# Placeholder rows written in bulk, rank products in another PSUM bank, a second buffer for turned tokens

## The chip, the cores and the metric

One core of a Trainium2 chip runs the whole program as one launch. The metric is device time in microseconds (us), the median of the runs of the kernel. The core has five engines: TensorE (PE in the profile), VectorE (DVE), ScalarE (ACT), GpSimd (POOL) and SyncE (SP). SP and POOL issue the DMAs, and these run on the core's 16 DMA engines.

## What is computed

The input is 8 images of 16 x 16 tokens with 192 channels, all in float32. Four blocks follow each other, each with a layer norm before it and a residual after it:

```
x = x + window_attention(ln(x))            # 14 x 14 windows, 12 heads, relative positions
t = t + gelu(ln(t) @ W_in + b) @ W_out      # dense feed-forward, 192 -> 768 -> 192
x = x + afno(ln(x))                         # rfft2, two block-diagonal complex layers, irfft2, plus a bias layer
t = t + moe(ln(t))                          # top 2 of 8 experts by softmax of gate logits
# moe: token -> its two experts' gelu(x @ w1[e] + b1[e]) @ w2[e] + b2[e], weighted by the two shares
```

## The kernel before, in words

The 2048 tokens are 16 tiles of 128 rows, in 4 groups of 4 tiles (GROUPS = 4; a group is two images). Every engine has its own instruction stream, written out by hand, and the streams meet only in semaphores. The order of the work is thus the order of the lines of each engine.

**Stages.** Attention comes first. The dense feed-forward stage is the loop with `hidden_layer` and `output_layer`. The AFNO stage is `forward`, `first_layer`, `second_layer`, `inverse` on PE, one pass for each group. The mixture-of-experts stage (MoE) overlaps it: while PE does group `it` of the AFNO stage, in `mixing(it)`, the gate of group `it - 1` is worked out. `turn_rows` and `gates` give the logits, DVE picks two experts for each token in `chosen` (a chain of small instructions in which each waits for the one before), `ranks` multiplies the 0/1 choice matrix by a triangular matrix and by ones to count tokens, and `slots` on DVE turns counts into slot numbers.

**The store of expert rows.** `xs_d` lies in HBM. It has a region of CAP = 2176 rows for each of the NE = 8 experts, and 128 more rows at FREE. A row has DX = 196 floats (784 B): 192 values of the token, its place and its shares. POOL's `scatter` (L596) writes every token's row to the slots of its two experts by indirect DMA, 8 DMAs for each group. Then each tile of 128 slots is an expert tile: SP loads it (`load_rows`, L475), PE turns it (`turn_x`, L1762), ACT copies the turned tile from PSUM bank 0 to `xst` (`turned`, L638), PE makes the first layer (`first`, L1793 and L1798), ACT the gelu (L801), PE the second layer (`second`, L1807), DVE bias and weight (`result`, L1257 to L1268), and POOL adds the 128 rows to the output in HBM by an indirect accumulating DMA (L623). There are NTILE = 39 such tiles. EARLY = 9 of them are started from the tokens of the first two groups, before the later groups have slots.

**Placeholder rows.** An expert's last tile is not full. Its rest must hold rows whose place points to a dump row of the output. Before the change, SP writes 128 placeholder rows behind the last taken slot of each expert, in `free_rows` (L477 to L480): it reads the slot from `next_i`, which DVE writes after the last group's slots (L1321), and copies 128 x 196 floats from the input `free_rows` to `xs_d`. These are 8 DMAs from HBM to HBM, four after the load of tile 6 and four after the load of tile 7. SP waits for them (`free_in`) ahead of the load of tile EARLY.

**Banks.** For groups 0 to 2 the gate's PSUM bank is 0 and the rank products lie in bank 1; for the last group they are banks 6 and 7. `turn_blocks` (L1592) writes banks 0 and 1, so PE waits for DVE's `slots` (g_slot) ahead of it in passes 1 and 2. `forward` writes banks 2 to 5.

**SP's order** around the change: small tables, then w1e and w2e of the eight experts (16 DMAs of some 577 KB, L457 and L458), b2e (L459), the dump rows of the output (L460), `store_residual(0)` and `(1)` (L465), a wait for the scatters of groups 0 and 1 (sc0), loads of tiles 0 to 3, `store_residual(2)` and `(3)`, loads of tiles 4 and on. **POOL's order**: scatter of groups 0, 1, 2, then the 39 additions, with the scatter of group 3 put between additions 2 and 4.

Of the kernel before, what the change touches and what calls it, by code (L numbers as in the profile page):

```python
# [13 lines left out]
I32 = mybir.dt.int32  # L14
ALU = mybir.AluOpType
# [32 lines left out]
NE = 8  # L48
# [24 lines left out]
def metaformer(nc, a, out):  # L73
    with ExitStack() as ctx:
# [140 lines left out]
        v8 = {n: down("e_" + n, [P, NE]) for n in ("next", "cnt", "full", "padded", "end", "begin", "taken", "start", "hop")}  # L215
        next_i = down("next_i", [P, NE], I32)
        above = down("above", [P, NE, 16])
# [12 lines left out]
        xtm = down("xtm", [C, 2, 512])  # L230
        xst = down("xst", [P, 2, P])

# [63 lines left out]
        def gate_bank(group):  # L296

            return 6 if group == GROUPS - 1 else 0


        @block.sync
        def _(sp):
# [153 lines left out]
            for e in range(NE):  # L456
                sp.dma_start(w1e[:, e, :], a["w1e"][:, e, :]).then_inc(s["w3_in"], 16)  # L457
                sp.dma_start(w2e[:, e, :, :], a["w2e"][:, e, :, :]).then_inc(s["w3_in"], 16)  # L458
            sp.dma_start(b2e[:].rearrange("p e d -> p (e d)"), a["b2e"].broadcast_to([P, NE * D])).then_inc(s["w3_in"], 16)  # L459
            sp.dma_start(out[NT], a["free_rows"][:, 0:D]).then_inc(s["res_out0"], 16)  # L460

# [14 lines left out]

            def free_rows(e):  # L477

                first = sp.value_load(next_i[0:1, e:e + 1], min_val=0, max_val=FREE - P)
                sp.dma_start(xs_d[ds(first, P), :], a["free_rows"]).then_inc(s["free_in"], 16)  # L480

            store_residual(0)
# [8 lines left out]
            for j in range(XB, EARLY):  # L491
                sp.wait_ge(s["e_ys"], 1 + j - XB + 1)
                load_rows(j, j % XB)
                if j == EARLY - 3:
                    sp.wait_ge(s["g_run"], GROUPS + 1)
                    for e in range(NE // 2):
                        free_rows(e)
                if j == EARLY - 2:
                    for e in range(NE // 2, NE):
                        free_rows(e)  # L500

            sp.wait_ge(s["g_tab"], 5)
            first = first_slot_of(EARLY)
            sp.wait_ge(s["free_in"], 16 * (NE + 1))
            sp.wait_ge(s["sc1"], 16 * NT)
# [17 lines left out]
        def _(pool):  # L523
# [69 lines left out]
            def scatter(group, tiles):  # L593
                for t in tiles:
                    for k in range(2):
                        nc.gpsimd.indirect_dma_start(  # L596
                            xs_d[:, :], bass.IndirectOffsetOnAxis(ap=slot_i[group][:, k, t:t + 1], axis=0),
                            rows[group][:, t, :], None).then_inc(s[f"sc{group // 2}"], 16)

            for group in range(GROUPS - 1):  # L600
                pool.wait_ge(s["g_slot"], 2 * group + 2)
                pool.wait_ge(s["g_col"], 4 * group + 4)
                scatter(group, range(4))
# [32 lines left out]
        def _(act):  # L636
# [166 lines left out]

            def turned(j):
                act.wait_ge(s["e_t"], j + 1)
                copy(xst[:], ps[:, 0, 0:2 * P].rearrange("p (c t) -> p c t", c=2), "e_xt")

            turned(0)
            root(GROUPS - 1)
            prepare(ACT.Gelu)  # L810
            turned(1)
            gelu(0, 0)
            turned_rows(GROUPS - 1, gate_bank(GROUPS - 1))
            turned(2)
            gelu(1, 1)
# [3 lines left out]
            for j in range(3, EARLY + 1):  # L819
                turned(j)  # L820
                gelu(j - 1, (j - 1) % 2)
            with act.Fori(2, (NTILE - 3) // XB) as it:
                for u in range(XB):
                    turned(XB * it + u + 2)
                    gelu(XB * it + u + 1, (u + 1) % 2)
            turned(NTILE - 1)
            gelu(NTILE - 2, (NTILE - 2) % 2)
# [4 lines left out]
        def _(dve):  # L832
# [316 lines left out]
            def slots(group):  # L1149

                dve.wait_ge(s["g_rank"], 2 * group + 2)
                link(group, nc.vector.tensor_copy(by_expert(g["tot"]),
                                                  ps[:, gate_bank(group) + 1, 4 * NE:8 * NE].rearrange("p (t e) -> p e t", e=NE)))
                link(group, nc.vector.tensor_tensor_scan(flat(g["cum"]), scan0[:].rearrange("p e t -> p (e t)"),
                                                         flat(g["tot"]), 0.0, ALU.mult, ALU.add))
                link(group, tt(flat(g["t"]), flat(g["cum"]), flat(g["tot"]), ALU.subtract))
                link(group, tt(g["slot"][:], by_expert(g["t"]).rearrange("p e t -> p t e"),
                               v8["next"][:].unsqueeze(1).broadcast_to([P, 4, NE]), ALU.add))
                link(group, tt(g["slot"][:], g["slot"][:],
                               ps[:, gate_bank(group) + 1, 0:4 * NE].rearrange("p (t e) -> p t e", e=NE), ALU.add))  # L1160
                for k, one in enumerate(("one1", "one2")):
                    link(group, tt(g["t"][:], g["slot"][:], g[one][:], ALU.mult))
                    link(group, red(v4[f"s{k + 1}"][:], g["t"][:], X, ALU.add))
                    nc.vector.tensor_copy(slot_i[group][:, k, :], v4[f"s{k + 1}"][:]).then_inc(s["g_slot"], 1)  # L1164
                tt(v8["next"][:], v8["next"][:], by_expert(g["cum"])[:, :, 3], ALU.add).then_inc(s["g_run"], 1)
# [153 lines left out]
            slots(last)  # L1319
            dve.wait_ge(s["g_run"], GROUPS)  # L1320
            nc.vector.tensor_copy(next_i[:], v8["next"][:]).then_inc(s["g_run"], 1)  # L1321
            early_result(2)
# [28 lines left out]
        def _(pe):  # L1351
# [308 lines left out]
            def forward(it):  # L1660

                pe.wait_ge(s["a_y2"], 1 + it * 4)
                for c in range(2):
                    for part in range(2):
                        for i in range(2):
                            for q in range(2):
# [64 lines left out]
            def ranks(group):  # L1731

                pe.wait_ge(s["g_both"], group + 1)
                both = g["both"][:].rearrange("p t e -> p (t e)")
                bank = gate_bank(group) + 1
                mm(ps[:, bank, 0:4 * NE], tri[:], both, start=True, stop=True).then_inc(s["g_rank"], 1)
                mm(ps[:, bank, 4 * NE:8 * NE], ones[:], both, start=True, stop=True).then_inc(s["g_rank"], 1)

            def mixing(it, more):
# [7 lines left out]
                second_layer(it)  # L1747
                inverse(it, 0)
                ranks(it - 1)
                if more:  # L1750
                    tokens_normal(GROUPS + 1 + it)
                    pe.wait_ge(s["g_slot"], 2 * it)
                    turn_blocks()
                else:
                    turn_x(0, 0, 16)
# [27 lines left out]
            def first(j, u, gelus):  # L1783
# [8 lines left out]
                for m in range(HT):  # L1792
                    mm(hidden(m), wst[:, u, m * P:(m + 1) * P], xst[:, 1 - m % 2, :], start=(m < 2), stop=False,  # L1793
                       skip_group_check=True)
                for m in range(HT):
                    r = slice(64 * (m % 2), 64 * (m % 2) + 64)
                    half = (HT + m // 2) * P
                    last = mm(hidden(m), wst[r, u, half:half + P], xst[r, m % 2, :], start=False, stop=True,  # L1798
                              skip_group_check=True)
# [9 lines left out]

            last = GROUPS - 1  # L1810
            for j in range(EARLY + 1):
                if j == 2:
                    gates(last)
                first(j, j % 2, HT * (j - 1) if j >= 2 else None)
                if j == 1:
                    turn_rows(last)
                turn_x(j + 1, (j + 1) % XB, 16 * ((j + 1) // XB + 1))
                if j == 3:
# [179 lines left out]
```

## Time and profile before

| what | value |
|---|---|
| runs shown | 661.95, 644.17, 640.72 us |
| median of them | 644.17 us |
| the profiled execution's own time | 644.17 us |
| its span, first to last instruction | 642.3 us |
| its mean granted TensorE clock | 0.908 |

The profile is of one execution. Its span is 1.87 us shorter than that execution's time, and that execution is also the median of the three. Engine times are busy times. Matmuls overlap, and their ends are modelled. "PEclk" or "clock" is the share of full TensorE speed that was granted: 1.00 is 2.4 GHz and 0.50 is 1.2 GHz. A DMA share of 1.00 means that all 16 DMA engines were busy.

### The profile page before, as it was taken

The page shows a single profiled execution, that of the slowest core. Times are in us where ns is not written, and L with a number is a line of the kernel's source. Part 1 is how long each engine was busy: PE and PEld are TensorE (multiplying, and loading weights), DVE is VectorE, ACT ScalarE, POOL GpSimd, SP SyncE. Part 2 cuts the span into 40 slices and gives each one's busy share as a digit, 9 for nine tenths or more (in the row PEclk, how much of TensorE's full clock was granted, in tenths as well). Part 3 has the DMA queues.
Part 4 walks back from the last instruction along what each step waited for, and adds up shares of the span by engine and source line. Part 5 has one row for each costly group of instructions (what it writes and reads, how often), then busy time and mean ns, then how long its engine had stood idle before and what let it go on. Part 6 is the DMA issues. An engine that isn't in the chain of part 4 may idle for free.

```text
span 642.3 us, 13223 instructions
## 1 busy us (share of the span) xinstructions
PE 572.9 (89%) x4624; PEld 475.8 (74%) x4625; DVE 298.2 (46%) x931; ACT 227.7 (35%) x572; POOL 129.6 (20%) x112
## 2 busy tenths in 40 slices
PE   1999998898899878999999988998949999999991
PEld 1778885666666656566688987887949999999991
DVE  6744436455776516422223636665724343443431
ACT  1123321244444443422232615245323434344440
POOL 8200100330000000000000040405444333323331
PEclk9999955578898889999999959698969999999997
DMA  7522686675556541880000020112332323232221
GB/s 207 104 70 57 192 198 132 139 205 85 85 84 87 84 85 25 341 323 1 0 1 1 26 75 1 63 38 83 71 88 39 51 37 49 43 44 44 42 37 13
DMA packets 33218, 53.81 MB, mean 84 GB/s; under 512 B 6645, under 2 KB 26733, under 8 KB 31654
## 3 DMA queue, kind: packets, MB, share of 16 engines
q1 hardware_dynamic: 25254, 43.64, 28.0%
q0 software_dynamic: 7920, 9.57, 8.6%
q8 instruction: 29, 0.48, 0.3%
q14 instruction: 15, 0.12, 0.1%
HBM read 33.05 MB, written 20.29 MB: 83 GB/s over the span
## 4 chain that ended last, share of the span: by engine, by line
PE 40%; issue 19%; DMA 8%; DVE 5%; ACT 5%; POOL 2%; POOLq 2%; DVEq 1%; SPq 0%; ACTq 0%
DMA out<-ys,place_i 7%; PE ps L1496 6%; PE ps L1640 4%; PE ps L1708 4%; PE ps L1627 3%; PE ps L1533 3%; PE ps L1487 2%; PE ps L1668 2%; PE ps L1631 2%; PE ps L1451 2%; POOLq L617 2%; PE ps L1675 1%; PE ps L1481 1%; POOL out L623 1%; ACT pt L698 1%
## 5 line engine op out<-in xcount | busy, mean ns | idle before, releaser
L623 POOL DMA_INDIRECT out<-ys,place_i x39 | 63.0, 1616 | 117.8 <-DVE ys L1268 109.2
L1807 PE MATMUL ps<-w2e,hts 128*128 x468 | 83.2, 328 | 1.5 <-DVE ys L1268 1.5
L1807 PEld LDWEIGHTS ps<-w2e,hts 128*128 128x128 f32 x468 | 75.6, 191 | 1.9 <-issue 1.8
L1793 PE MATMUL ps<-xst,wst 128*128 128x128 f32 x468 | 60.9, 282 | 11.2 <-issue 11.2
L1793 PEld LDWEIGHTS ps<-xst,wst 128*128 128x128 f32 x468 | 59.0, 197 | 11.7 <-issue 11.6
L596 POOL DMA_INDIRECT xs_d<-rows,slot_i x32 | 32.0, 999 | 166.5 <-DVE slot_i L1164 157.6
L801 ACT ACTIVATE hts<-ps,wst 128x128 f32<-128x128 f32 x234 | 64.4, 382 | 2.0 <-PE ps L1798 2.0
L698 ACT ACTIVATE pt<-ps 98x392 f32<-98x392 f32 x96 | 42.5, 495 | 45.2 <-PE ps L1496 45.2
L942 DVE TENSOR_REDUCE negm<-ps 98x2 f32<-98x392 f32 x96 | 48.4, 548 | 20.5 <-PE ps L1451 20.3
L1496 PE MATMUL ps<-qa,ka 48*98 48x196 f32 x384 | 47.9, 371 | 6.3 <-ACT pt L698 3.4
L638 ACT ACTIVATE xst<-ps 128x256 f32<-128x256 f32 x39 | 14.9, 383 | 108.4 <-PE ps L1762 95.8
L1257 DVE TENSOR_TENSOR yb<-ps,b2e 128x192 f32<-128x192 f32 x39 | 13.9, 357 | 84.9 <-PE ps L1807 76.0
L1496 PEld LDWEIGHTS ps<-qa,ka 48*98 48x98 f32 x384 | 30.7, 176 | 14.7 <-ACT pt L698 8.9
L1249 DVE COPY wst<-w1e 128x1158 f32 x39 | 30.2, 777 | 22.4 <-issue 20.8
L1002 DVE TENSOR_TENSOR x<-x,ps 128x384 f32<-128x384 f32 (+1 forms) x24 | 13.2, 550 | 58.9 <-PE ps L1640 44.6
L1798 PE MATMUL ps<-xst,wst 64*128 64x128 f32 x468 | 38.0, 297 | 0.0
L1798 PEld LDWEIGHTS ps<-xst,wst 64*128 64x128 f32 x468 | 30.4, 194 | 4.9 <-issue 0.4
L1640 PEld LDWEIGHTS ps<-wout,ht 128*128 128x128 f32 x192 | 31.0, 190 | 3.0 <-issue 3.0
L1640 PE MATMUL ps<-wout,ht 128*128 128x192 f32 x192 | 32.9, 328 | 0.0
L1451 PE MATMUL ps<-kb,qb 48*98 48x196 bf16 x192 | 28.0, 296 | 4.5 <-DVE negm L942 2.0
L638 ACT ACTIVATE xf<-ps 64x288 f32<-64x288 f32 x32 | 12.9, 404 | 51.0 <-PE ps L1668 32.2
L1708 PE MATMUL ps<-y,idft 72*128 72x192 f32 x128 | 29.0, 379 | 0.7 <-DVE y L1063 0.5
(224 smaller groups left out, 950.0 us busy)
## 6 DMA issues: line engine op xcount, KB each, us to landing
w1e<-in_w1e SPq DMA_DIRECT2D x8, 579.0 KB, 11.3
w2e<-in_w2e SPq DMA_DIRECT2D x8, 576.0 KB, 12.2
xs<-xs_d SPq DMA_DIRECT2D x39, 98.0 KB, 1.9
ka<-k_d SPq DMA_DIRECT2D x12, 170.0 KB
k_d<-kst SPq DMA_DIRECT2D x16, 121.5 KB, 1.9
x<-in_xp SPq DMA_DIRECT2D x4, 384.0 KB, 5.9
q_d<-qt SPq DMA_DIRECT2D x2, 768.0 KB, 5.6
qa<-q_d SPq DMA_DIRECT2D x12, 128.0 KB
```

What stands on the lines that cost most here:

```text
L596: nc.gpsimd.indirect_dma_start(xs_d[:, :], bass.IndirectOffsetOnAxis(ap=slot_i[group][:, k, t:t + 1], axis=0), rows[group][:, t, :], None) ...
L623: nc.gpsimd.indirect_dma_start(acc, bass.IndirectOffsetOnAxis(ap=place_i[:, j % 2:j % 2 + 1], axis=0), ys[:, j % 2, :], None, compute_op=A ...
L698: nc.scalar.activation(dst, src, ACT.Exp).then_inc(s["t_exp"], 1)
L801: nc.scalar.activation(hts[:, u, m, :], ps[:, 1 + 2 * u + m % 2, m // 2 * P:(m // 2 + 1) * P], ACT.Gelu, bias=wst[:, u, W1W - HT + m:W1W - ...
L942: nc.vector.tensor_reduce(dst, src, X, ALU.max, negate=True).then_inc(s["m_red"], 1)
L1451: last = mm(ps[0:98, bank, q * WIN:(q + 1) * WIN], qb[head(e), n, b * TOK + 98 * q:b * TOK + 98 * q + 98], kb[head(e), n, key_cols(b):key_ ...
L1496: last = mm(ps[0:98, banks[e], k * WIN:(k + 1) * WIN], ka[head(e), n, key_cols(b) + 98 * k:key_cols(b) + 98 * k + 98], qa[head(e), n, b * ...
L1640: last = mm(ps[:, 6 + half, (k % 2) * D:(k % 2 + 1) * D], ht[:, m, k * P:(k + 1) * P], wout[:, m, :], start=(m == 0), stop=(m == HT - 1))
L1708: last = mm(ps[:, 6 + i, q * D:(q + 1) * D], idft[:, f, r, q * P:(q + 1) * P], y2[:, i, f, :].rearrange("p (n r d) -> p n r d", n=4, r=2)[ ...
L1793: mm(hidden(m), wst[:, u, m * P:(m + 1) * P], xst[:, 1 - m % 2, :], start=(m < 2), stop=False, skip_group_check=True)
L1798: last = mm(hidden(m), wst[r, u, half:half + P], xst[r, m % 2, :], start=False, stop=True, skip_group_check=True)
L1807: last = mm(ps[:, 5, 0:D], hts[:, u, k, :], w2e[:, ds(e, 1), k, :], start=(k == 0), stop=(k == HT - 1))
```

## The change

There are three edits.

1. The placeholder rows are written once, in bulk. SP issues 8 DMAs right behind b2e, each for a whole region of 2176 rows, as 17 blocks of 128 rows: the destination is seen as `(t p) d -> t p d` with t = 17, the source is the same 128 rows with a new front axis repeated 17 times. POOL waits for all of them ahead of its first scatter. `free_rows`, `next_i`, its copy on DVE and SP's late wait are gone.
2. The rank products of groups 0 to 2 go to bank 5. PE no longer waits for `slots` ahead of `turn_blocks`; it waits for them ahead of the last quarter of the next `forward`, and for all four AFNO biases of the group ahead of `ranks`.
3. `xst` has two buffers. PE turns tile 1 ahead of `first(0)`, and ACT copies it ahead of `root` of the last group.

```
-        next_i = down("next_i", [P, NE], I32)
-        xst = down("xst", [P, 2, P])
+        xst = down("xst", [P, 2, 2, P])
+        def rank_bank(group):
+            return 7 if group == GROUPS - 1 else 5
 # SP
             sp.dma_start(b2e[:]...).then_inc(s["w3_in"], 16)
+            for e in range(NE):
+                sp.dma_start(xs_d[e * CAP:(e + 1) * CAP, :].rearrange("(t p) d -> t p d", p=P),
+                             a["free_rows"].unsqueeze(0).broadcast_to([CAP // P, P, DX])).then_inc(s["free_in"], 16)
             sp.dma_start(out[NT], a["free_rows"][:, 0:D]).then_inc(s["res_out0"], 16)
-            def free_rows(e):
-                first = sp.value_load(next_i[0:1, e:e + 1], min_val=0, max_val=FREE - P)
-                sp.dma_start(xs_d[ds(first, P), :], a["free_rows"]).then_inc(s["free_in"], 16)
-                if j == EARLY - 3:
-                    sp.wait_ge(s["g_run"], GROUPS + 1)
-                    for e in range(NE // 2):
-                        free_rows(e)
-                if j == EARLY - 2:
-                    for e in range(NE // 2, NE):
-                        free_rows(e)
-            sp.wait_ge(s["free_in"], 16 * (NE + 1))
 # POOL
+            pool.wait_ge(s["free_in"], 16 * (NE + 1))
             for group in range(GROUPS - 1):
                 pool.wait_ge(s["g_slot"], 2 * group + 2)
 # ACT
-            turned(0)
+            turned(0, 0)
+            turned(1, 1)
             root(GROUPS - 1)
             prepare(ACT.Gelu)
-            turned(1)
             gelu(0, 0)
 # DVE: slots() reads rank_bank(group); after slots(last):
-            dve.wait_ge(s["g_run"], GROUPS)
-            nc.vector.tensor_copy(next_i[:], v8["next"][:]).then_inc(s["g_run"], 1)
 # PE, forward(it)
                     for part in range(2):
+                        if it > 1 and c and part:
+                            pe.wait_ge(s["g_slot"], 2 * (it - 1))
 # PE, mixing(it)
                 inverse(it, 0)
+                pe.wait_ge(s["a_y2"], 1 + it * 4 + 4)
                 ranks(it - 1)
                 if more:
                     tokens_normal(GROUPS + 1 + it)
-                    pe.wait_ge(s["g_slot"], 2 * it)
                     turn_blocks()
 # PE, expert tiles: first() reads xst[:, u]
+            turn_x(1, 1, 16)
             for j in range(EARLY + 1):
                 first(j, j % 2, HT * (j - 1) if j >= 2 else None)
-                turn_x(j + 1, (j + 1) % XB, 16 * ((j + 1) // XB + 1))
+                if j:
+                    turn_x(j + 1, (j + 1) % XB, 16 * ((j + 1) // XB + 1))
```

## Rows read from the trace of the kernel before

**Rows 1.** The page: busy time, granted clock and GB/s in 40 slices of the span.

```profile
PE 572.9 (89%) x4624; PEld 475.8 (74%) x4625; DVE 298.2 (46%) x931; ACT 227.7 (35%) x572; POOL 129.6 (20%) x112
PEclk9999955578898889999999959698969999999997
GB/s 207 104 70 57 192 198 132 139 205 85 85 84 87 84 85 25 341 323 1 0 1 1 26 75 1 63 38 83 71 88 39 51 37 49 43 44 44 42 37 13
```

**Rows 2.** Windows of the span: busy us and count by engine, clock, DMA share, GB/s.

```profile
core 0: us, PE busy (x) PEld busy (x) DVE busy (x) ACT busy (x) POOL busy (x), PEclk, DMA share, GB/s
262.00:282.00 20.00, 19.74 (x86) 12.53 (x88) 4.83 (x22) 6.69 (x12) 0.00 (x0) 1.00 1.02 412
290.00:330.00 40.00, 39.57 (x190) 27.27 (x190) 9.59 (x37) 11.48 (x20) 0.00 (x0) 1.00 0.00 1
371.00:386.00 15.00, 14.08 (x60) 14.11 (x61) 4.42 (x23) 2.60 (x7) 7.94 (x8) 0.56 0.24 80
401.00:414.00 13.00, 12.31 (x55) 12.35 (x56) 8.70 (x48) 0.81 (x2) 7.76 (x8) 0.61 0.18 62
466.00:474.00 8.00, 0.00 (x0) 0.00 (x0) 0.00 (x0) 0.28 (x1) 5.44 (x5) 0.73 0.45 113
474.00:481.00 7.00, 6.79 (x36) 6.37 (x37) 4.11 (x17) 3.32 (x14) 1.95 (x1) 0.58 0.36 71
500.00:560.00 60.00, 60.00 (x506) 56.74 (x506) 24.35 (x83) 25.19 (x92) 20.66 (x13) 1.00 0.29 43
```

**Rows 3.** PE's waits for another engine, 365 to 415: us in total, times, longest.

```profile
PE ps L1592 <- DVE slot_i L1164: 5.0, 2, 2.5
```

**Rows 4.** PE in order of time: start, us, group, and idle time before it.

```profile
429.21 0.41 PE L1762 MATMUL ps<-ident,xs 128*128 128x128 f32 x2
...
438.29 2.35 PE L1793 MATMUL ps<-xst,wst 128*128 128x128 f32 x12 [2.75 <-issue]
...
474.21 2.90 PE L1793 MATMUL ps<-xst,wst 128*128 128x128 f32 x12 [8.40 <-issue]
```

**Rows 5.** DVE in order of time: the last instruction of the early table.

```profile
407.58 0.17 DVE L1227 TENSOR_TENSOR e_hop<-e_hop,e_taken 128x7 f32<-128x7 f32 x1
```

**Rows 6.** DMA packets in 111.2:111.5, 141.4:141.8, 95.2:97.5, 287.3:330, in this order.

```profile
DMA packets 12, 0.00 MB, mean 6 GB/s; under 512 B 12, under 2 KB 12, under 8 KB 12
...
DMA packets 16, 0.01 MB, mean 16 GB/s; under 512 B 8, under 2 KB 16, under 8 KB 16
...
DMA packets 117, 0.39 MB, mean 167 GB/s; under 512 B 28, under 2 KB 28, under 8 KB 112
...
DMA packets 2, 0.03 MB, mean 1 GB/s; under 512 B 0, under 2 KB 0, under 8 KB 0
```

**Rows 7.** POOL in order of time: the first scatter of group 0, the last of group 1.

```profile
372.07 1.11 POOL L596 DMA_INDIRECT xs_d<-rows,slot_i  x1 [117.59 <-DVE slot_i L1164]
...
410.74 0.97 POOL L596 DMA_INDIRECT xs_d<-rows,slot_i  x1 [0.30 <-issue]
```

**Rows 8.** SP's queue in 381.5:383.4, then all packets and SP's queue in 474.2:475.2.

```profile
q1 hardware_dynamic: 528, 0.39, 66.9%
...
DMA packets 32, 0.10 MB, mean 100 GB/s; under 512 B 16, under 2 KB 16, under 8 KB 32
q1 hardware_dynamic: 32, 0.10, 48.6%
```

**Rows 9.** GB/s in 40 slices of 262:282.

```profile
GB/s 387 378 434 389 408 397 406 396 416 426 417 406 433 424 398 435 458 369 406 406 407 426 425 397 424 407 426 417 397 424 397 435 417 389 434 406 416 426 398 425
```

**Rows 10.** SP's DMA issues in order of time: start, us, line, copy, count.

```profile
270.95 2.03 SPq L460 DMA_DIRECT2D out<-in_free_rows  x1
...
353.14 28.13 SPq L465 DMA_DIRECT2D out<-x  x2
...
414.18 3.74 SPq L475 DMA_DIRECT2D xs<-xs_d  x4
```

More of the change, by code:

```diff
@@ L802, in gelu, with turned @@
                                          ACT.Gelu, bias=wst[:, u, W1W - HT + m:W1W - HT + m + 1]).then_inc(s["e_g"], 1)
-            def turned(j):
+            def turned(j, u):
                 act.wait_ge(s["e_t"], j + 1)
-                copy(xst[:], ps[:, 0, 0:2 * P].rearrange("p (c t) -> p c t", c=2), "e_xt")
-            turned(0)
+                copy(xst[:, u], ps[:, 0, 0:2 * P].rearrange("p (c t) -> p c t", c=2), "e_xt")
+            turned(0, 0)
+            turned(1, 1)
             root(GROUPS - 1)
             prepare(ACT.Gelu)
-            turned(1)
             gelu(0, 0)
             turned_rows(GROUPS - 1, gate_bank(GROUPS - 1))
-            turned(2)
+            turned(2, 0)
             gelu(1, 1)
@@ L819, in _ @@
             for j in range(3, EARLY + 1):
-                turned(j)
+                turned(j, j % 2)
                 gelu(j - 1, (j - 1) % 2)
@@ L823, in _ @@
                 for u in range(XB):
-                    turned(XB * it + u + 2)
+                    turned(XB * it + u + 2, u % 2)
                     gelu(XB * it + u + 1, (u + 1) % 2)
-            turned(NTILE - 1)
+            turned(NTILE - 1, (NTILE - 1) % 2)
             gelu(NTILE - 2, (NTILE - 2) % 2)
@@ L1152, in slots @@
                 link(group, nc.vector.tensor_copy(by_expert(g["tot"]),
-                                                  ps[:, gate_bank(group) + 1, 4 * NE:8 * NE].rearrange("p (t e) -> p e t", e=NE)))
+                                                  ps[:, rank_bank(group), 4 * NE:8 * NE].rearrange("p (t e) -> p e t", e=NE)))
                 link(group, nc.vector.tensor_tensor_scan(flat(g["cum"]), scan0[:].rearrange("p e t -> p (e t)"),
@@ L1159, in slots @@
                 link(group, tt(g["slot"][:], g["slot"][:],
-                               ps[:, gate_bank(group) + 1, 0:4 * NE].rearrange("p (t e) -> p t e", e=NE), ALU.add))
+                               ps[:, rank_bank(group), 0:4 * NE].rearrange("p (t e) -> p t e", e=NE), ALU.add))
                 for k, one in enumerate(("one1", "one2")):
@@ L1734, in ranks @@
                 both = g["both"][:].rearrange("p t e -> p (t e)")
-                bank = gate_bank(group) + 1
+                bank = rank_bank(group)
                 mm(ps[:, bank, 0:4 * NE], tri[:], both, start=True, stop=True).then_inc(s["g_rank"], 1)
@@ L1792, in first @@
                 for m in range(HT):
-                    mm(hidden(m), wst[:, u, m * P:(m + 1) * P], xst[:, 1 - m % 2, :], start=(m < 2), stop=False,
+                    mm(hidden(m), wst[:, u, m * P:(m + 1) * P], xst[:, u, 1 - m % 2, :], start=(m < 2), stop=False,
                        skip_group_check=True)
@@ L1797, in first @@
                     half = (HT + m // 2) * P
-                    last = mm(hidden(m), wst[r, u, half:half + P], xst[r, m % 2, :], start=False, stop=True,
+                    last = mm(hidden(m), wst[r, u, half:half + P], xst[r, u, m % 2, :], start=False, stop=True,
                               skip_group_check=True)
```

## The prediction, written before the changed kernel had run

> **What bounds the kernel now.** I read the page first, then the windows of single stages, then waits and order of time where a window showed idle time, and last the DMA packets. On the page the reader is to see that PE is the busy engine (89% of the span), that its clock is below full in a few slices, and that the DMA engines are nearly unused between slices 18 and 22 [rows 1]. The windows say which stretches cost time: from 500 to 560 us PE is busy all 60 us at full clock, so the expert tiles are bound by PE; from 371 to 386 and from 401 to 414 it has a clock of 0.56 and 0.61; from 466 to 474 it does nothing at all [rows 2]. PE's waits name the cause of the first two: ahead of `turn_blocks` it waits 2.5 us for DVE's slots, twice [rows 3]. In order of time two more gaps stand: 2.75 us ahead of `first(1)` at 438.29, where ACT copies tile 1 only after `root` and a table load, and 8.40 us ahead of `first(6)` at 474.21 [rows 4]. In that last gap SP is in its placeholder copies and POOL in the last scatters; the profile names no engine as its cause.
>
> The profiled execution took 644.17 us, 1.87 more than its span of 642.3, and is itself the median of the runs shown. I add 1.9 to each span.
>
> **Edit 2, the rank products.** It removes both waits of 2.5 us [rows 3] and, with them, most of the slow clock behind. A clock of 0.56 over 15 us means that (1 - 0.56) x 2 x 15 = 13.2 us ran at 1.2 GHz, where half, 6.6 us, is lost; 0.61 over 13 us gives 10.1 and 5.1 us [rows 2]. With the waits that is 16.7 us at most. In pass 2 the early table on DVE ends at 407.58 [rows 5], and the token rows that PE turns next come behind it, some 5 us later; PE would reach that turn about 4 us before they are ready. So the second saving is largely given back, and I take 11 us, between 6 (the first pass alone, with a cold clock again) and 17. The new wait on `a_y2` costs nothing: DVE writes all four biases before the choice matrix that `ranks` waits for anyway. The new wait in `forward` asks for slots that are a whole inverse transform old. Both counts hold only if PE goes on to something; see below what takes all of it away.
>
> **Edit 3, two buffers.** The 2.75 us ahead of `first(1)` go [rows 4], with the half clock of `first(1)` itself (12 matmuls took 2.35 us there). What is late next is `turn_rows` of the last group (its rows are ready near 438) and then the gelu of tile 0, behind the table load. I take 4 us, between 0 and 6. `root` is not later: its variances come some 7 us after PE turned tile 0.
>
> **Edit 1, what goes.** The 8 copies, the copy to `next_i` and SP's wait go from the tile loop. If the copies cause the gap of 8.40 us [rows 4], it goes too, with the slow clock of 0.58 over the next 7 us (2.9 us lost) [rows 2]: 11 us. If not, 0. No row decides it; I take 11, since nothing else is new in that stretch, and 0 stays an end.
>
> **Edit 1, what comes.** The bulk copies write 8 x 17 x 128 x 784 B = 13.65 MB, a quarter of what the whole program moves. Where they run there is room: from 290 to 330 us the DMA share is 0.00 [rows 2], and from 287.3 to 330 there are 2 packets in all [rows 6]. The first scatter, at 372.07, needs them [rows 7]. So there are 85 us of cover, if all 16 DMA engines take part. That is the question on which everything hangs.
>
> How a copy is spread can be counted in the trace. Each DMA engine that takes part closes its share with one small packet, under 512 B. A copy of 8 rows of 784 B has 16 packets, 8 of them under 512 B: 8 closings. A copy of 8 rows of 240 B from 4 partitions has 12 packets: 4 closings. The window over the ends of two copies of 84 rows (8 and 4 KB each) has 28 packets under 512 B: 14 closings each, not 16 [rows 6]. A residual store over 128 partitions has 528 packets in its window, 512 rows and 16 closings, and one placeholder copy of before has 32: 16 pieces of 6272 B and 16 closings [rows 8]. So 4, 8, 14, 16 and 16 engines for outer counts of 4, 8, 84, 128 and 16: each time the largest number up to 16 that divides the outer count. The old copy was one contiguous block, which could be cut into 16. The new one has a source that repeats 17 times; that axis can't be merged with the 128 rows behind it, and 17 has no divisor up to 16 but 1. I read it so that each bulk copy runs on one DMA engine, and all eight on the same one, one after the other.
>
> The Trainium skill ("DMA: Bandwidth & Descriptors", section on why a DMA increments its semaphore by 16) states the same as a rule: the largest k up to 16 that divides the slowest dimension that isn't 1 of both sides, and on SP's queue always the lowest k engines. The trace agrees for five shapes and has none with 17. By that page the copies take one engine and the change loses; without it the five counts alone say so.
>
> What one engine moves: from 262 to 282 us all 16 are busy (share 1.02) at 412 GB/s, which is 25.75 GB/s for one [rows 2]. 13.65 MB at that rate is 530 us. This is for loads from HBM to SBUF. For HBM to HBM the nearest row is one old copy: 0.10 MB at 48.6% of 16 engines over 1.0 us, 7.8 engine-us, 12.9 GB/s [rows 8], with 16 engines starting on the same 98 KB at once. That bound is 1058 us. The lower bound is the best slice of the load stage, 458 GB/s over 16 engines, 28.6 GB/s, 477 us [rows 9]. I take 530, since an engine alone with long pieces is nearer to the streaming row.
>
> **The sum for one engine.** The weights keep the engines busy until 287 [rows 6], so the last placeholder lands at 287 + 530 = 817 us. Queued behind POOL's wait: the scatters of groups 0 to 2 and all 39 additions. SP's wait for the scatters of groups 0 and 1 stands ahead of the loads of tiles 0 to 3, and PE's turn of tile 0 behind these, inside pass 3. SP's residual stores (353.14) have a share behind the bulk copies on the same engine and land with them, before anyone needs them [rows 10]. PE does everything up to the turn of tile 0 and stops. Edit 2's saving lies wholly in front of that stop and is worth nothing.
> From the release to the turn of tile 0: 16 scatters. Each takes 0.97 us and 0.30 of issue, so 15 x 1.27 = 19.1 us from first to last, 0.4 more to start, then 414.18 - 410.74 = 3.4 us until the load is issued [rows 7, 10], and some 2 us to land and turn: 25 us. The turn is at 817 + 25 = 842.
> From the turn of tile 0 to the end the trace has 642.3 - 429.2 = 213.1 us [rows 4]. Off it come 4 (edit 3) and 11 (the gap); on it go 4 for PE's cold clock after a stop of over 400 us, a little under the 5 to 7 us that the stretches at 0.56 and 0.61 lost. That is 202 us. Span 842 + 202 = 1044; time 1046 us.
> Own range of this case: 477 instead of 530 gives 993; a copy rate of 24 GB/s gives 569 and 1085; a gap that stays gives 11 more. So 995 to 1100; the 1058 us bound would give about 1575, to which I give little.
>
> **Rivals.** (a) All 16 engines take part, because the copy is emitted with another outer count than 17. Against it: the source's repeated axis; for it: the old copy was cut into 16. Then 13.65 MB at 412 GB/s take 33 us, or 66 at 12.9 GB/s for each of 16, over by 353, before the first scatter: hidden. Time: 644.2 - 11 - 4 - 11 = 618 us (629 if the gap stays).
> (b) Spread over 16, but HBM to HBM copies stop PE as in the 8.40 us gap [rows 4]. This is the rival on the slower side that does not need 17: its place is the dense feed-forward stage, its price at most the copies' own 33 to 66 us, during which PE would get little done, and it decides from 26 us on, the sum of the savings. With 45 us: 644 - 26 + 45 = 663. Against it: PE is busy 19.74 of 20 us beside loads at 412 GB/s [rows 2], though these write to SBUF.
> (c) The change does less than it says: bulk copies hidden, the gap has another cause, PE waits for DVE instead of for slots (6 us) and for the gelu instead of tile 1 (1 us). 644 - 7 = 637 us.
>
> **How the numbers follow.** One engine 0.66, (a) 0.22, (b) 0.07, (c) 0.05. A measurement of this kernel tells about 2% from no change, 631 to 657 us. Faster: (a), 0.22. Within 2%: (c) and the milder end of (b), 0.07. Slower: the rest, 0.71. The likeliest case gives 1046 us. Its own range holds some 0.57, so for 8 in 10 the whole range must reach (a) as well: 612 to 1100, which leaves out the slow tail of one engine and the ends of (a).
>
> **What would show it.** One engine: from 290 to 800 the DMA share stands near 1/16 (0.06) at about 26 GB/s, each bulk copy leaves 1 closing packet where 16 would be, POOL idles from 255 to about 815, PE stops near 420 at L1762 and resumes 25 us after POOL starts; the clock is at half as it resumes. Sixteen engines: a share near 1 right behind the weights, and POOL's first scatter near 370. Edit 2: no wait of L1592 for slot_i, clock 1.00 there. Edit 3: no gap ahead of `first(1)`. The gap: `first(6)` follows the second layer of tile 4 at once. The forecast is wrong if the share behind the weights is far above 0.06; its size is wrong if one engine moves much less than 25 GB/s from HBM to HBM.

## The result, and the profile after

The kernel with the three edits takes 1038.95 us (median of 4 runs, 1031.57 to 1043.76) against 644.07 us (640.72 to 661.95) for the kernel before: a ratio of 1.614, with a 95% interval of 1.602 to 1.625. It is slower, by about 395 us. The forecast was 1046 us. The profiled execution took 1040.92 us, with a span of 1039.1. The ratios of this document compare undisturbed executions only, so they are not exactly the ratios of the medians.

The page of the kernel after, in the parts that answer to [rows 1], with the row of DMA busy tenths and one of its DMA issues:

```profile
PE 585.8 (56%) x4624; PEld 479.5 (46%) x4625; DVE 298.9 (29%) x930; ACT 227.7 (22%) x572; POOL 128.2 (12%) x112
PEclk9995557885999999955555555555555579999998
DMA  7247634463280000000000000001010132333321
GB/s 189 61 132 170 149 115 74 82 88 61 89 339 28 28 29 28 30 27 27 27 27 27 27 27 27 27 31 41 27 41 27 67 86 64 51 42 46 46 41 20
...
xs_d<-in_free_rows SPq DMA_DIRECT2D x8, 1666.0 KB
```

PE has nearly as many busy us as before (585.8 against 572.9), so nearly nothing was added to its work. The time is a hole: counted from 0, the granted clock is 0.5 in slices 17 to 31. From slice 12 to slice 30 the DMA engines move 27 to 31 GB/s, with 41 twice. That row is the whole story in one line: a store of rows being filled at the speed of one of 16 engines.

The windows, to be read beside [rows 2] (us, busy time and count by engine, clock, DMA share, GB/s):

```profile
280.00:308.00 28.00, 26.17 (x113) 15.66 (x112) 9.75 (x37) 9.11 (x16) 0.00 (x0) 1.00 0.95 373
310.00:350.00 40.00, 40.00 (x188) 27.05 (x184) 8.10 (x33) 12.61 (x21) 0.00 (x0) 1.00 0.07 28
500.00:800.00 300.00, 0.00 (x0) 0.00 (x0) 0.00 (x0) 0.00 (x0) 0.00 (x0) 0.50 0.07 30
800.00:830.00 30.00, 0.00 (x0) 0.00 (x0) 0.00 (x0) 0.00 (x0) 15.20 (x16) 0.50 0.17 60
830.00:850.00 20.00, 14.75 (x83) 14.08 (x84) 4.09 (x17) 4.22 (x12) 8.19 (x9) 0.61 0.36 106
900.00:960.00 60.00, 60.00 (x504) 56.86 (x503) 23.51 (x78) 26.15 (x96) 20.64 (x13) 1.00 0.31 45
```

The weights come in at full DMA width until about 307. Then the share drops to 0.07, about one sixteenth, and stays there for some 500 us; from 500 to 800 PE, DVE, ACT and POOL are not busy at all. When it is over, the expert tiles run as before: 60 of 60 us of PE, 504 matmuls where there were 506, full clock.

The waits of the whole span, one row for each engine that stops (us in total, times, longest):

```profile
POOL xs_d L589 <- DMA xs_d<-in_free_rows: 534.3, 1, 534.3
ACT xst L632 <- PE ps L1756: 502.0, 38, 402.4
DVE x L996 <- PE ps L1702: 404.8, 4, 398.5
...
PE ps L1756 <- DMA xs<-xs_d: 396.3, 1, 396.3
```

Only the first of these rows is a cause. POOL waits for the placeholder rows; PE's turn of tile 0 (L1756) waits for a load that needs POOL's scatters; ACT and DVE wait for PE. The chain in order of time, first POOL, then PE:

```profile
275.72 0.20 POOL L583 MEMSET ones<- 128x128 f32 x1 [55.26 <-DMA ao<-ot]
810.23 1.11 POOL L589 DMA_INDIRECT xs_d<-rows,slot_i  x1 [534.30 <-DMA xs_d<-in_free_rows]
...
829.48 0.97 POOL L589 DMA_INDIRECT xs_d<-rows,slot_i  x1 [0.30 <-issue]
```

```profile
438.52 0.39 PE L1731 MATMUL ps<-g_both,ones 128*128 128x32 f32 x2
835.25 0.69 PE L1756 MATMUL ps<-ident,xs 128*128 128x128 f32 x2 [396.35 <-DMA xs<-xs_d]
```

In [rows 7] the same first scatter started at 372.07, released by DVE's slots. Now it starts at 810.23. From it to PE's turn of tile 0 there are 25.0 us.

Two DMA windows count the engines that take part. 320 to 380, then 380 to 500:

```profile
DMA packets 35, 1.64 MB, mean 27 GB/s; under 512 B 1, under 2 KB 1, under 8 KB 1
...
DMA packets 73, 3.34 MB, mean 28 GB/s; under 512 B 2, under 2 KB 2, under 8 KB 2
```

In 180 us there are 3 small closing packets. A region of 1.706 MB at 27.1 GB/s takes 63 us, so this is one closing for each copy; one placeholder copy of the kernel before had 16 [rows 8].

### The profile page after: what moved, and what is told of

Its sections match the earlier page's. It is cut to its first block, busy times and chain, and to the rows that moved or that the text cites. A ratio compares the mean times of both kernels' runs of the same rounds, so it can differ in the third digit from the quotient of the medians.

```text
span 1039.1 us, 13183 instructions
## 1 busy us (share of the span) xinstructions
PE 585.8 (56%) x4624; PEld 479.5 (46%) x4625; DVE 298.9 (29%) x930; ACT 227.7 (22%) x572; POOL 128.2 (12%) x112
## 4 chain that ended last, share of the span: by engine, by line
issue 51%; PE 25%; DMA 4%; POOL 3%; ACT 2%; DVE 2%; POOLq 1%; SPq 0%; ACTq 0%; DVEq 0%
PE ps L1488 5%; DMA out<-ys,place_i 3%; PE ps L1632 3%; PE ps L1525 2%; PE ps L1619 2%; POOL xs_d L589 2%; PE ps L1479 2%; PE ps L1702 1%; PE ps L1623 1%; PE ps L1443 1%; POOLq L611 1%; PE ps L1473 1%; POOL out L617 1%; PE ps L1787 1%; PE ps L1801 1%
## 5 line engine op out<-in xcount | busy, mean ns | idle before, releaser
L1756 PE MATMUL ps<-ident,xs 128*128 128x128 f32 x78 | 17.5, 307 | 396.4 <-DMA xs<-xs_d 396.3
L1756 PEld LDWEIGHTS ps<-ident,xs 128*128 128x128 f32 x78 | 8.2, 144 | 401.0 <-DMA xs<-xs_d 396.7
L1488 PE MATMUL ps<-qa,ka 48*98 48x196 f32 x384 | 59.3, 442 | 5.3 <-ACT pt L692 2.7
L1488 PEld LDWEIGHTS ps<-qa,ka 48*98 48x98 f32 x384 | 37.6, 216 | 17.4 <-ACT pt L692 10.5
```

What stands on the lines that cost most here:

```text
L1488: last = mm(ps[0:98, banks[e], k * WIN:(k + 1) * WIN], ka[head(e), n, key_cols(b) + 98 * k:key_cols(b) + 98 * k + 98], qa[head(e), n, b * ...
```

## The experiments

Because whole executions of this kernel differ by some 20 us (more on that at the end), I compare stretches and not only times. All start from one instruction, POOL's memset of `ones` (at 275.72 above), which every kernel has right ahead of SP's issues of the expert weights. Worked out from the traces of one execution each; the first two columns count in us from that memset, the others are lengths in us:

| kernel | first scatter | turn of tile 0 | between them | turn of tile 0 to the end |
|---|---|---|---|---|
| before | 117.8 | 174.9 | 57.1 | 213.1 |
| before, second profile (e9) | 123.2 | 180.7 | 57.5 | 204.7 |
| edit 1 spread, alone (e3) | 120.7 | 178.9 | 58.2 | 203.6 |
| edit 2 alone (e4) | 121.3 | 170.1 | 48.9 | 206.4 |
| edit 3 alone (e5) | 118.1 | 166.3 | 48.2 | 201.5 |
| edits 2 and 3 (e2) | 122.8 | 167.8 | 44.9 | 202.2 |
| edits 2 and 3, spread bulk and late copies (e8) | 118.8 | 163.3 | 44.5 | 201.3 |
| all edits, 16 engines (e1) | 118.6 | 163.2 | 44.6 | 199.8 |
| the same again (e10) | 121.8 | 170.1 | 48.3 | 199.7 |
| all edits, blocks of 16 and 1 (e11) | 118.6 | 166.4 | 47.8 | 199.6 |
| all edits, outer count 4 (e6) | 159.8 | 185.4 | 25.6 | 203.8 |
| all edits, outer count 2 (e7) | 283.7 | 309.0 | 25.3 | 204.1 |
| after (outer count 17) | 534.5 | 559.5 | 25.0 | 203.8 |

The same kernel (e1 and e10) differs by 3.2 us up to the first scatter and by 3.7 us between the scatter and the turn, so such a difference in these columns is not yet an effect. From the turn of tile 0 to the end the two agree to 0.1 us.

**How many engines.** The first question was whether the outer count of the copy alone makes the 395 us. The same rows go to the same places; only the cut differs. `q` is the outer count. In the cuts of code the `.then_inc(s["free_in"], 16)` behind each copy is left out.

```
-                sp.dma_start(xs_d[e * CAP:(e + 1) * CAP, :].rearrange("(t p) d -> t p d", p=P),
-                             a["free_rows"].unsqueeze(0).broadcast_to([CAP // P, P, DX]))
+                sp.dma_start(xs_d[e * CAP:(e + 1) * CAP, :].rearrange("(t q r) d -> q t (r d)", q=16, r=P // 16),
+                             a["free_rows"].rearrange("(q r) d -> q (r d)", q=16).unsqueeze(1).broadcast_to(
+                                 [16, CAP // P, P // 16 * DX]))
```

> The changed kernel with one thing altered: each bulk copy has an outer count of 16 (16 blocks of 8 rows, each repeated 17 times) for the same 13.65 MB. If the number of DMA engines sets the price, the copies take 35 to 65 us behind the weights, are done before 372 us, and the time is 618 us (610 to 632). If the volume from HBM to HBM sets it, whatever the spread, the time stays near 1039 us. If spread copies stop PE in the dense feed-forward stage, it is 640 to 670 us and PE shows gaps between 290 and 350.

Measured: 630.36 us (median of 4, 620.78 to 651.66), with 645.18 (635.53 to 660.42) for the kernel before beside it. That lies inside the expected 610 to 632, at its upper end, 12 us above the 618. The hole is gone.

Then the same edit with q=4 and q=2:

> The same copies with an outer count of 4: 126 us, to about 415 to 430 us, some 10 us later than the slots of group 1; the turn of tile 0 comes near 440 to 455 instead of 420: 645 us (635 to 665), DMA share 0.25. By volume alone: 1039 us.

> The same copies with an outer count of 2. Two engines at 27 GB/s each take 252 us behind the weights, to about 540 to 560; then 25 us to the turn of tile 0 and 204 to the end: 770 us (755 to 795), DMA share 0.13. By volume alone: 1039 us.

Measured, one execution each: 649.93 us for four and 773.75 us for two, both inside the expected ranges and far from the 1039 us that the volume alone would give. POOL's first scatter, for four, then for two:

```profile
418.68 1.11 POOL L590 DMA_INDIRECT xs_d<-rows,slot_i  x1 [159.62 <-DMA xs_d<-in_free_rows]
```

```profile
542.51 1.11 POOL L590 DMA_INDIRECT xs_d<-rows,slot_i  x1 [283.52 <-DMA xs_d<-in_free_rows]
```

And the window 290 to 310 of outer count 4, 2 and 16, where the copies run in all three:

```profile
290.00:310.00 20.00, 20.00 (x88) 12.27 (x85) 4.67 (x14) 6.15 (x10) 0.00 (x0) 1.00 0.26 110
```

```profile
290.00:310.00 20.00, 20.00 (x88) 12.25 (x86) 5.60 (x17) 4.88 (x8) 0.00 (x0) 1.00 0.13 55
```

```profile
290.00:310.00 20.00, 20.00 (x95) 13.38 (x92) 3.60 (x10) 6.15 (x10) 0.00 (x0) 1.00 1.02 311
310.00:330.00 20.00, 19.98 (x95) 13.68 (x93) 4.55 (x24) 6.47 (x11) 0.00 (x0) 1.00 0.95 294
```

Shares of 0.07, 0.13, 0.26 and 1.02 are 1, 2, 4 and 16 engines. The first scatter stands at 534.5, 283.7 and 159.8 us after the memset. From one engine to two it moves by 250.8, from two to four by 123.9, half as much, as bytes over engines should. With 16 the copies are no longer what POOL waits for: the row of e11 below, and that of e1 in the same way (118.40 us), name DVE's slots. PE is busy for all 20 us beside copies of 311 GB/s, so rival (b), that copies within HBM stop PE, falls.

**The number or the repetition.** A source that is read 17 times could fall on one engine whatever the number is. One more kernel keeps the shape of the change and makes the number 16; the 17th block is a copy of its own.

```
-                sp.dma_start(xs_d[e * CAP:(e + 1) * CAP, :].rearrange("(t p) d -> t p d", p=P),
-                             a["free_rows"].unsqueeze(0).broadcast_to([CAP // P, P, DX]))
+                sp.dma_start(xs_d[e * CAP:(e + 1) * CAP - P, :].rearrange("(t p) d -> t p d", p=P),
+                             a["free_rows"].unsqueeze(0).broadcast_to([CAP // P - 1, P, DX]))
+                sp.dma_start(xs_d[(e + 1) * CAP - P:(e + 1) * CAP, :], a["free_rows"])
```

> The changed kernel with the copy of each region cut in two: 16 of its 17 blocks in one copy of the very shape of the change (the same source repeated along a new front axis, now 16 times), the 17th block in a copy like the old one. Theory (the outer count of 17 is at fault): outer count 16, so all 16 engines take part; with the 31 to 50 us that the spread copies took for the same bytes, the first scatter waits for slots at about 118 us after POOL's memset and the time is 618 to 650 us. Rival (a source that repeats, or a front axis of long blocks, falls on one engine whatever its count): the first scatter at about 510 to 535 us after the memset and 1010 to 1040 us.

Measured: 625.21 us (one execution). The first scatter of this kernel, and its windows under the copies:

```profile
375.86 1.11 POOL L590 DMA_INDIRECT xs_d<-rows,slot_i  x1 [118.42 <-DVE slot_i L1159]
```

```profile
290.00:310.00 20.00, 20.00 (x90) 12.48 (x89) 3.60 (x10) 5.58 (x10) 0.00 (x0) 1.00 1.05 334
310.00:330.00 20.00, 20.00 (x97) 13.99 (x96) 3.44 (x19) 7.26 (x13) 0.00 (x0) 1.00 0.96 300
```

The scatter stands where it was expected, and the time lies inside the expected 618 to 650. The repetition does no harm; the 17 does. The whole loss hangs on one block more than 16.

**The parts one by one.** Edit 2 and edit 3 each alone, both with the old late copies, and the kernel before once more, all on one chip. Their diffs are parts of the change shown above. Edit 3 alone:

> Edit 3 alone (two buffers of turned tokens). The 2.75 us ahead of first(1) go; worth 4 us (0 to 6): the stretch from the memset of ones is 384 us with the gap or 373 without.

Edit 2 alone:

> Edit 2 alone (rank products in bank 5). No wait of PE for slot_i ahead of turn_blocks and clock 1.00 there. By the prediction it is worth 11 us (6 to 17): the stretch from the memset of ones is 377 us with the gap or 366 without. The changed kernel's passes came every 21.1 us instead of 27.8 and 29.3, which speaks for 14 to 15.

Both, with the old copies:

> Edits 2 and 3 alone; the placeholder rows are written as before. Savings of 11 and 4 us by the prediction: from POOL's memset of ones to the end 373 us (388.0 less 15) with the gap, 362 without. Since the kernel with both kinds of copies showed no gap, I expect none: 362 to 366.

The kernel before again, unchanged:

> The kernel before, unchanged, for a second profile. From the end of the attention stage (POOL's memset of ones) to the end the first profile has 388.0 us. If the 8.4 us gap ahead of first(6) belongs to this kernel, it stands again and the stretch is 386 to 390 us. If it was a single event, the gap is missing and the stretch is 11 us shorter, 376 to 379.

Measured, one execution each, in this order: 646.58, 637.2, 629.94 and 663.14 us. The times alone would mislead: the kernel before had 663.14 here and 631.58 in an execution beside it. The stretches say more. The waits are where the prediction put them. PE in order of time, edit 2 alone, and the kernel before again:

```profile
412.11 1.91 PE L1725 MATMUL ps<-ident,rows 128*96 128x128 f32 x8 [4.56 <-DVE rows L1107]
```

```profile
398.96 1.06 PE L1592 MATMUL ps<-ident,xnp 128*128 128x128 f32 x8 [2.49 <-DVE slot_i L1164]
...
429.04 1.06 PE L1592 MATMUL ps<-ident,xnp 128*128 128x128 f32 x8 [2.49 <-DVE slot_i L1164]
...
465.64 2.90 PE L1793 MATMUL ps<-xst,wst 128*128 128x128 f32 x12 [2.75 <-ACT xst L638]
...
498.66 1.50 PE L1793 MATMUL ps<-xst,wst 128*128 128x128 f32 x12
```

With edit 2 both waits of 2.49 us for slots are gone, and a wait of 4.3 to 4.6 us for DVE's token rows stands in the last pass. A shorter one was there already: 1.9 us in e9, e3 and e5, 0.6 in the first profile. With edit 3 the 2.75 us are gone.

The sizes missed. From the memset to the end e5 has 367.8 us (373 expected without the gap), e4 376.5 (366), e2 370.0 (362 to 366) and e9 385.4 (376 to 379). One reason is the base: I had taken 11 us off it for the gap, but e9 has no such gap and is only 2.6 us shorter than the first profile. Against e9 the savings are 17.6, 8.9 and 15.4 us, with 4, 11 and 15 forecast. The 17.6 us are not edit 3's alone: 5.1 lie ahead of the first scatter and 9.3 between it and the turn of tile 0, and edit 3 changes nothing that runs in either; 3.3 lie behind the turn.

The last row of the kernel before again is the surprise: this is the first layer of tile 6, and it has no gap ahead of it. The late copies stand at the same place in SP's stream:

```profile
487.38 5.10 SPq L480 DMA_DIRECT2D xs_d<-in_free_rows  x4
493.26 0.36 SPq L475 DMA_DIRECT2D xs<-xs_d  x1
494.39 4.39 SPq L480 DMA_DIRECT2D xs_d<-in_free_rows  x4
```

So the 8.40 us of [rows 4] are not a price that the late copies always have. None of the profiles of e2, e4, e5, e8 and e9 has them, and all five kernels make those copies. Six profiles with late copies, one of them with the gap, can't rule out that the copies bring it now and then; its cause stays open. In the first profile PE turned the next tile at 463.41, and ACT, idle for 12.43 us, copied it only 10 us later, where the tile before took 0.5 us (458.88 to 459.36). POOL went on scattering.

```profile
463.41 0.44 PE L1762 MATMUL ps<-ident,xs 128*128 128x128 f32 x2
...
473.73 0.38 ACT L638 ACTIVATE xst<-ps 128x256 f32<-128x256 f32 x1 [12.43 <-remote]
```

So not PE alone stood still. What the late copies do have in each of those five profiles is PE waiting for the loads of two expert tiles, 1.4 to 2.4 us in sum; e1, e3, e10 and e11, without late copies, have no such wait. In the kernel before again:

```profile
495.61 0.44 PE L1762 MATMUL ps<-ident,xs 128*128 128x128 f32 x2 [0.46 <-DMA xs<-xs_d]
...
501.96 0.44 PE L1762 MATMUL ps<-ident,xs 128*128 128x128 f32 x2 [0.92 <-DMA xs<-xs_d]
```

**Bulk copies and late copies together.** To price the late copies by themselves, e8 is e1 with them put back, with `next_i` and its copy on DVE.

```
...
+                if j == EARLY - 3:
+                    sp.wait_ge(s["g_run"], GROUPS + 1)
+                    for e in range(NE // 2):
+                        free_rows(e)
+                if j == EARLY - 2:
+                    for e in range(NE // 2, NE):
+                        free_rows(e)
...
+            sp.wait_ge(s["free_in"], 16 * (2 * NE + 1))
```

> The kernel of e1_sixteen with the 8 late copies of the kernel before put back, at their old places and with their wait; they write again what is there. If they cause the 8.4 us gap ahead of first(6), it is back and the time is 8 to 12 us over e1_sixteen (near 629). If the gap has another cause, both agree within 3 us, and the gap stands in neither or in both.

Measured: 639.46 us (median of 12, 622.15 to 659.9), a ratio of 0.977 to the kernel before (0.968 to 0.987). The medians of e8 and e1 lie 9.1 us apart, where 8 to 12 was the sign expected of the gap; but the profile of e8 has no gap there. From the turn of tile 0 to the end it needs 201.3 us and e1 199.8: in these two profiles the late copies cost 1.5 us.

**Edit 1 alone, spread.**

> The kernel before with edit 1 alone, its copies cut by 16: no late copies, the old banks and the single buffer. Theory: the bulk copies lie under the dense feed-forward stage and the late copies cost some 1.5 us, so the stretch from POOL's memset of the ones to the end is that of the kernel before without its gap of 8.40 us, 385 us less 1 to 2, and the two waits of L1592's turn and the 2.75 us ahead of the first layer of tile 1 are there again. Rival (the 8.40 us gap belongs to the late copies after all): it is seen in no execution of this kernel, but then would be seen in most of those with them.

Measured: 655.4 us (one execution), 382.5 us from the memset to the end, against 385.4 in the second profile of the kernel before. The two waits of 2.49 us and the 2.75 us are there, as expected. Of the 2.9 us between them, 2.5 lie ahead of the first scatter (120.7 against 123.2), where POOL waits for slots in both; between the scatter and the turn e3 is 0.7 us longer; 1.1 lie behind the turn of tile 0, where the late copies were. Edit 1 by itself is worth about 1 us once it is spread.

**All three edits, spread.** The kernel of e1 again, in more executions:

> All three edits, with the bulk copies cut by 16 row groups instead of by 17 blocks; the same kernel as e1_sixteen, timed against the kernel before in more rounds. Theory: edit 2 brings 9 to 13 us and edit 3 brings 3 to 4, so 12 to 17 us less than before, a ratio of 0.974 to 0.981. Rival (the two waits only moved, and what e8_both showed was chance): a ratio of 0.99 to 1.00.

Measured: 631.27 us (median of 6, 623.15 to 640.88) against 648.79 (641.66 to 669.01), a ratio of 0.969 with a 95% interval of 0.960 to 0.979. The theory's 0.974 to 0.981 lies partly in it, the rival's 0.99 to 1.00 does not. The three edits together make the kernel faster, if the bulk copies are cut so that all engines take part; by how much, between 2 and 4%, is less sure.

## Why the prediction was right

**The cause.** The step on which everything hung was the reading from closing packets that an outer count of 17 means one engine. The runs bear it out for four outer counts: 17 gives one engine, 2 two, 4 four, 16 sixteen; and e11 shows that the number, not the repeated source, is the cause. The rule of the Trainium skill ("DMA: Bandwidth & Descriptors", section on why a DMA increments its semaphore by 16) says the same; the shares of 0.07, 0.13, 0.26 and 1.02 agree with it.

**The sum, term by term.**

| term | forecast | measured |
|---|---|---|
| the weights end | 287 | 308 |
| the bulk copies | 530 us | 502 us |
| POOL is released | 817 | 810.2 |
| release to the turn of tile 0 | 25 us | 25.0 us |
| turn of tile 0 to the end | 202 us | 203.8 us |
| span | 1044 | 1039.1 |

That the span came within 5 us of the forecast is in part luck: two terms were off by more than 20 us and offset each other. The weights came 21 us later, because the attention stage took longer in this execution (the memset stands at 275.7 instead of 254.3); that has nothing to do with the change. And one engine moved 27.1 GB/s instead of 25.75: 13.65 MB took 28 us less. My row was a sixteenth of what 16 engines did together, and an engine alone is a little faster than that. The bound of 12.9 GB/s, from one small copy, was far off; the choice against it was right.

**The tail was right by its size, with one term misread.** I took 213.1 - 4 - 11 + 4 = 202. The runs show: an execution of the kernel before without the 8.40 us gap has 204.7. Edit 3 takes off 3.3 (e9 against e5), 4.2 (e4 against e2) or 3.9 (e3 against e10); forecast 4. Without the late copies it is 1.1 to 2.4 shorter (e3 against e9, e1 against e8 and e2). That gives 198 to 200; e1, e10 and e11 have 199.6 to 199.8. The kernel after has 203.8, 4.0 more, and 4 was forecast for the cold clock. The clock is enough for it: in the first 10 us from the turn of tile 0 the kernel after has a granted clock of 0.50 and 36 matmuls, e1 has 1.00 and 84. The length of the stop doesn't show in it: e6, where PE stopped for 15.35 us instead of 396, has the same 0.50, 36 and 203.8. The term that didn't hold is the 11 us for the gap. The copies by themselves are worth 1.1 to 2.4, and the gap was seen in one execution only; together they make 9.5 to 10.8, so the 11 came out near by its size and not by its reason. The half clock behind the gap is real in the trace (27 matmuls in 5 us at 0.50, against 43 in the same time later), but between the two profiles of the kernel before it doesn't show as a loss: 213.1 - 204.7 = 8.4, the gap alone, since e9 has the 1.4 us of waits for tile loads instead, and other differences that I haven't separated.

**What was hidden.** Edit 2 was said to lie in front of PE's stop and to be worth nothing. In the kernel after, PE went idle at 438.9 and stood still for 396 us. I had written that it would stop near 420. Counted from the memset it is 163.2 us, which in the first profile of the kernel before would be 417; it is the later start that puts it at 439. From one `forward` to the next it took 21.1 us twice, where the kernel before took 27.7 and 29.8 (the text of e4 has 27.8 and 29.3, and the trace doesn't show the second); from the last `forward` to `ranks` it took 22.1 instead of 19.0, with the wait for DVE's rows in it. So the giving back in the last pass was there too.

**Edit 2 where it counts.** Forecast 11 us, 6 to 17. From the first scatter to the turn of tile 0, three executions without edit 2 have 57.1 to 58.2 us; the six with edit 2 and 16 engines or late copies have 44.5 to 48.9, on average 46.5. That is 11.1 us. But there is a fourth without edit 2, e5, and it has 48.2 us; with it the difference of the averages is 8.8 us. What is late next was named rightly: DVE's token rows, about 4 us, measured 4.3 to 4.6. e5 shows that most of the gain is not the wait. Edit 3 alone keeps both waits of 2.49 us, and its clock behind the first of them stays full, where the second profile of the kernel before shows 0.68. The window behind that wait in the kernel before again, and in e5:

```profile
398.00:414.00 16.00, 15.04 (x73) 14.76 (x74) 6.39 (x30) 4.41 (x11) 7.92 (x8) 0.68 0.22 75
```

```profile
394.00:410.00 16.00, 15.06 (x107) 13.79 (x108) 7.58 (x36) 9.20 (x21) 7.93 (x8) 1.00 0.23 76
```

PE is busy for 15.0 us in both, and does 73 matmuls in one and 107 in the other. Where the clock stayed full behind the old waits, edit 2 is worth 3.3 us (e5 48.2, e2 44.9); the rest of the 11 goes with the half clock that followed the first old wait in three executions of four. What decides whether it follows stays open. So the 11 us are right as a size for this mix of executions, and the worth of edit 2 in a single one lies anywhere from nothing (e5 48.2, e4 48.9) to 14 us (e3 58.2, e8 44.5). Behind the longer wait for token rows a half clock can stand as well: edit 2 alone is at half clock behind it, 38 matmuls in 10 us.

```profile
412.00:422.00 10.00, 9.89 (x38) 9.12 (x39) 2.11 (x12) 6.93 (x14) 0.00 (x0) 0.50 0.28 81
```

The windows of 10 us behind that wait have 0.50, 0.50 and 0.55 in e4, e10 and e11, which need 48 to 49 us in the stretch, and 0.83, 0.84 and 0.83 in e1, e2 and e8, which need 44.5 to 45.

**Rival (a)** named 618 us for 16 engines; measured were 630.36 and 631.27 as medians, 620.78 as the fastest. It took the 11 us of the gap as a gain, and without these it would have said 629, as it noted. **Rival (c)**, 637 us or a ratio of 0.989, lies outside the interval of e10 (0.960 to 0.979) and falls for the spread kernel. Its doubt on the gap was right; its doubt on edit 3 (1 us) was wrong, 3.3 to 4.2 measured; its doubt on edit 2 (6 us) holds where the clock is full behind the old waits.

## What to carry to other kernels

Ask of each new DMA by how many engines it can be moved, before asking where its bytes are hidden. In every copy counted here it was the largest number up to 16 that divides the outermost axis, so 17 blocks went to one engine, and one block split off (17 = 16 + 1), or a cut along an inner axis, gave back 16. The small closing packets in a DMA window count the engines of a copy, and counts from copies already in the trace can tell what a new shape will get; pieces of the copy that are themselves small must be told apart from them. And a gap that stands in one profile, without a releaser, is to be seen in a second profile before it is given to a cause: here 8.40 us of idle time beside the suspected copies were gone in the next execution, with the copies in place.

## What was not expected of the hardware

**Bandwidth inside HBM grows less than the number of engines.** 27 GB/s for one engine, 55 for two, 110 for four, but a mean of 301 from 300 to 330 us for sixteen with pieces of 6 KB (e1), and 310 in the same window with most of the bytes in pieces of 50 KB (e11). That is 19 GB/s for each, against 27. Loads of weights from HBM to SBUF reached 412 [rows 2]. Where between 4 and 16 it bends was not measured.

**The issuing engine is held too.** SP's own part in the bulk copies, in the kernel after:

```profile
291.85 324.71 SPq L464 DMA_DIRECT2D xs_d<-in_free_rows  x8
616.61 70.20 SPq L466 DMA_DIRECT2D out<-in_free_rows  x1
686.86 72.08 SPq L471 DMA_DIRECT2D out<-x  x2
```

and in e1 and, for the first copy of 16 blocks and the block behind it, in e11:

```profile
272.50 31.12 SPq L464 DMA_DIRECT2D xs_d<-in_free_rows  x8
```

```profile
273.61 2.11 SPq L464 DMA_DIRECT2D xs_d<-in_free_rows  x1
275.76 0.66 SPq L466 DMA_DIRECT2D xs_d<-in_free_rows  x1
```

Eight issues took SP 324.71 us with one engine, 108.96 with two (e7), 61.09 with four (e6) and 31.12 with sixteen and 6 KB pieces. In e11, sixteen issues (from 273.61 to 285.3) took 11.7. I had let SP issue freely and only the data come late. Here nothing urgent stood behind them: SP was through at 758.9, before POOL was released. A load for another stage in that place would have been issued late.

**Most of the scatter of the times lies in the attention stage.** POOL's memset starts at 254 to 259 us in eight of the profiled executions (before, e1, e2, e4, e6, e7, e10, e11) and at 271 to 277 in the other five. The window 180 to 240 of the first profile of the kernel before, then of the second:

```profile
180.00:240.00 60.00, 52.65 (x762) 36.20 (x758) 31.31 (x64) 27.43 (x64) 2.09 (x4) 0.91 0.52 84
```

```profile
180.00:240.00 60.00, 56.34 (x582) 36.74 (x578) 29.11 (x58) 20.19 (x48) 2.08 (x4) 0.60 0.43 71
```

It is the same code with a clock of 0.91 and of 0.60, and 762 against 582 matmuls in the same time. What decides between the two is open; no run looked for it. Between these two profiles the memset moved by 21.6 us and the span by 19.0. So single times of this kernel can't price an edit of 10 us. The stretches behind the memset are better, but not free of it: e1 and e10, the same kernel, have 363.0 and 369.8 us from the memset to the end.
